# First cross attention: scores of two pairs of heads at a time, or of four

## The reference, cut to what matters

```python
q = _split_heads(Q @ Wq + bq)            # Q: layernorm of x, (16, 64, 512); 16 heads of 32
k = _split_heads(K @ Wk + bk)            # K, V: the context, (16, 512, 512)
v = _split_heads(V @ Wv + bv)
logits = einsum('bhqd,bhkd->bhqk', q, k) / sqrt(32) + mask * -1e9
attn = softmax(logits, axis=-1)
ctx = einsum('bhqk,bhkd->bhqd', attn, v).transpose(0, 2, 1, 3).reshape(Q.shape[0], Q.shape[1], DIM)
return ctx @ Wo + bo
```

## Time and profile before

| what | value |
|---|---|
| time, median of 3 runs (lowest, highest) | 1757.63 us (1753.8, 1759.28) |
| the profiled execution: its own time | 1758.54 us |
| its span in the profile | 1756.8 us |
| its granted TensorE clock, mean | 0.942 of full speed |
| PE busy, DVE busy, ACT busy over the span | 1528.7, 1122.2, 591.7 us |
| first cross attention's main loop | from 92 to 664 us of the span |

### The profile page before, as it was taken

How to read it: one execution, slowest core, us unless ns; L and a number is a source line. 1 busy time by engine, 2 the same in 40 slices (tenths; PEclk the granted TensorE clock), 3 DMA queues, 4 the chain that set the end, 5 groups by cost and what they waited for, 6 DMA issues and landing times. The chain is left out here.

```text
span 1756.8 us, 34069 instructions
## 1 busy us (share of the span) xinstructions
PE 1528.7 (87%) x14116; PEld 996.4 (57%) x14130; DVE 1122.2 (64%) x2155; ACT 591.7 (34%) x1221; POOL 295.8 (17%) x185
## 2 busy tenths in 40 slices
PE   6789999999999994998577899998799995895786
PEld 3567777777777763344545344444466663585343
DVE  3257667676676765521975757675488883765575
ACT  1244443443434442132023110111466662044332
POOL 0400000000000000310010000000499992160000
PEclk9889999999999997899888899998899997998899
DMA  6113122231222204000005000000455421004001
GB/s 231 61 39 132 64 84 86 75 126 70 83 80 90 75 19 158 0 0 1 4 2 198 1 0 0 0 0 0 186 178 191 169 99 35 1 3 145 0 0 48
DMA packets 47909, 120.05 MB, mean 68 GB/s; under 512 B 10605, under 2 KB 15469, under 8 KB 43674
## 3 DMA queue, kind: packets, MB, share of 16 engines
q1 hardware_dynamic: 47770, 118.04, 19.6%
HBM read 100.95 MB, written 17.07 MB: 67 GB/s over the span
## 5 line engine op out<-in xcount | busy, mean ns | idle before, releaser
L1130 POOL TENSOR_TENSOR tm_mixed<-tm_mixed,XNT 128x512 f32<-128x512 f32 x16 | 21.8, 1382 | 662.1 <-DVE tm_mixed L1153 662.1
L617 ACT ACTIVATE l0x_ctxT<-l0x_upper 128x512 fp32r<-128x512 f32 x64 | 40.4, 631 | 237.4 <-DVE l0x_ctxT_lower L700 237.4
L478 PE MATMUL bank<-l0x_ctxT,l0x_upper_k 128*128 128x512 f32 x256 | 104.7, 409 | 5.1 <-ACT l0x_upper_k L627 5.1
L697 DVE TENSOR_SCALAR l0x_upper<-bank 128x512 int32<-128x512 int32 x64 | 44.0, 688 | 95.2 <-PE bank L460 90.6
L478 PE MATMUL bank<-l0x_upper_v,l0x_ctxT 128*128 128x512 f32 x256 | 102.6, 401 | 0.0
L478 PE MATMUL bank<-l0x_ctxT,l0x_lower_k 128*128 128x512 f32 x256 | 101.5, 396 | 0.0
L478 PE MATMUL bank<-l0x_ctxT_lower,l0x_upper_k 128*128 128x512 f32 x256 | 101.4, 396 | 0.0
L478 PE MATMUL bank<-l0x_upper_v,l0x_ctxT_lower 128*128 128x512 f32 x256 | 100.6, 393 | 0.0
L478 PE MATMUL bank<-l0x_lower_v,l0x_ctxT 128*128 128x512 f32 x256 | 100.5, 392 | 0.0
L709 DVE CUSTOM_DVE_ANT_0 l0x_prob<-bank,l0x_mask 128x512 f32<-128x512 f32 x128 | 83.1, 687 | 21.2 <-PE bank L489 20.9
L1043 DVE TENSOR_REDUCE l1x_negmax<-bank 128x1 f32<-128x512 f32 x128 | 82.4, 686 | 21.2 <-PE bank L932 20.8
(11 more groups left out here) (264 smaller groups left out, 3373.5 us busy)
## 6 DMA issues: line engine op xcount, KB each, us to landing
l0x_ctx<-in_ctx SPq DMA_DIRECT2D x16, 1024.0 KB, 5.3
l1x_ctx<-in_ctx SPq DMA_DIRECT2D x16, 1024.0 KB, 5.8
fp_weight<-l0x_weight_piece SPq DMA_DIRECT2D x24, 352.0 KB, 2.4
f_raw<-fp_weight SPq DMA_DIRECT2D x3, 2816.0 KB, 17.4
ternary_weight<-l1x_piece_out SPq DMA_DIRECT2D x24, 256.0 KB, 6.1
f_raw<-ternary_weight SPq DMA_DIRECT2D x3, 2048.0 KB, 14.1
l0x_abs_piece<-in_L_ffn_w_gate SPq DMA_DIRECT2D x8, 512.0 KB, 5.7
l0x_mask<-mask_scratch SPq DMA_DIRECT2D x16, 256.0 KB, 3.6
```

The lines of the kernel that those rows point to most:

```text
L478: last = nc.tensor.matmul(work[bank][:, :], stationary, moving, start=kc == 0 and i == 0, stop=kc == CH - 1 and i == 2)
L697: nc.vector.tensor_scalar(upper.bitcast(I32), work[bank][:, :].bitcast(I32), UPPER_BITS, None, ALU.bitwise_and).then_inc(ctx_upper, 1)
```

## The change

- `scores` issues the four pairs of a half batch at once, on all four row groups: eight products, 16 records, into four banks. It is called in odd steps only. Before, a call had four products and stood in every step.
- The banks come from elsewhere: `score` has four, `probt` one (was two), `pv` one (was two).
- With one `probt` bank, the second pair's four transposes follow the first pair's copy. They are issued behind the step's first projection; ACT's copy, exponential and key copy are interleaved pair by pair likewise.
- `masked_scores` waits once per half batch for scores, and, as PE no longer orders it, for the transposes that read the probabilities which it overwrites.
- With one `pv` bank, `half_product` of step 2 waits for `finish_heads` of the batch before it, not of the one before that.

```diff
-    score, probt, pv, work = g.bank[0:2], g.bank[2:4], g.bank[4:6], g.bank[6:8]
+    score, probt, pv, work = g.bank[0:4], g.bank[4], g.bank[5], g.bank[6:8]
...
-            def scores(b, s):
+            def scores(b, half):
                 par, tokens = b % 2, slice(b * T, (b + 1) * T)
+                if b + half > 0:
+                    pe.wait_ge(masked, (2 * b + half) * 4)
                 for e in range(2):
-                    for i in range(2):
-                        half, r = s // 2, 2 * (s % 2) + i
+                    for r in range(4):
                         rows = slice(32 * r, 32 * r + 32)
-                        last = nc.tensor.matmul(score[i][e * T:(e + 1) * T, :], w.QT[rows, 2 * half + e, tokens],
+                        last = nc.tensor.matmul(score[r][e * T:(e + 1) * T, :], w.QT[rows, 2 * half + e, tokens],
                                                 w.KT[par][rows, 2 * half + e, :], start=True, stop=True)
...
-                        if not (last and u1 == 2):
+                        if s % 2 == 1 and not (last and u1 == 2):
                             if s1 == 0:
                                 pe.wait_ge(key_ready, b0 * CH + CH * (u1 + 1))
-                            pe.wait_ge(masked, n + 2)
-                            scores(b0 + u1, s1)
+                            scores(b0 + u1, s1 // 2)
...
-                                if not first:
-                                    pe.wait_ge(heads_done, b0 + (u - 1))
+                                if not (first and u == 0):
+                                    pe.wait_ge(heads_done, b0 + u)
...
                         for i in range(2):
+                            p = 2 * s + i
                             pe.wait_ge(exp_done, n + (i + 1))
-                            if not (first and u == 0 and s == 0):
-                                pe.wait_ge(probt_ready, n + (i - 1))
+                            if not (first and u == 0 and s == 0 and i == 0):
+                                pe.wait_ge(probt_ready, n + i)
                             for kc in range(KC):
-                                ins = nc.tensor.transpose(probt[i][:, kc * P:(kc + 1) * P],
+                                ins = nc.tensor.transpose(probt[:, kc * P:(kc + 1) * P],
                                                           w.prob[2 * (s % 2) + i][:, kc * P:(kc + 1) * P], g.ident[:, :])
                             ins.then_inc(probt_full, 1)
-                        for p in (2 * s, 2 * s + 1):
                             if ("project", u, p) in uses:
...
-                            nc.scalar.activation(w.PT[r][:, :], probt[i][:, :], ACT.Copy).then_inc(probt_ready, 1)
-                        if not (last and u1 == 2):
-                            exponentials(n + 2, u1 % 2, s1)
-                        for p in (2 * s, 2 * s + 1):
+                            nc.scalar.activation(w.PT[r][:, :], probt[:, :], ACT.Copy).then_inc(probt_ready, 1)
+                            if not (last and u1 == 2):
+                                exponential(n + 2, u1 % 2, s1, i)
                             if ("project", u, p) in uses and p < CH:
...
-                        dve.wait_ge(score_full, m + 1)
+                        dve.wait_ge(score_full, m // 2 + 1)
+                        if m >= 2:
+                            dve.wait_ge(probt_full, 2 * m - 2)
```

More of the change, by code:

```diff
@@ L498, in half_product @@
                             h = head_of(half, e, r)
-                            last = nc.tensor.matmul(pv[par][32 * r:32 * r + 32, (2 * half + e) * T:(2 * half + e + 1) * T],
+                            last = nc.tensor.matmul(pv[32 * r:32 * r + 32, (2 * half + e) * T:(2 * half + e + 1) * T],
                                                     w.V[par][:, kc, h * HD:(h + 1) * HD],
@@ L503, in half_product, with turn_sums @@
                 last.then_inc(half_full, 1)
-            def turn_sums(par):
+            def turn_sums():
                 for half in range(2):
-                    last = nc.tensor.transpose(pv[par][:, 256 + half * P:256 + (half + 1) * P],
+                    last = nc.tensor.transpose(pv[:, 256 + half * P:256 + (half + 1) * P],
                                                w.spread[:, half * P:(half + 1) * P], g.ident[:, :])
@@ L579, in body @@
                             pe.wait_ge(spread_done, b0 + u)
-                            turn_sums(1 - u)
+                            turn_sums()
                         for i in range(2):
+                            p = 2 * s + i
                             pe.wait_ge(exp_done, n + (i + 1))
-                            if not (first and u == 0 and s == 0):
-                                pe.wait_ge(probt_ready, n + (i - 1))
+                            if not (first and u == 0 and s == 0 and i == 0):
+                                pe.wait_ge(probt_ready, n + i)
                             for kc in range(KC):
-                                ins = nc.tensor.transpose(probt[i][:, kc * P:(kc + 1) * P],
+                                ins = nc.tensor.transpose(probt[:, kc * P:(kc + 1) * P],
                                                           w.prob[2 * (s % 2) + i][:, kc * P:(kc + 1) * P], g.ident[:, :])
                             ins.then_inc(probt_full, 1)
-                        for p in (2 * s, 2 * s + 1):
                             if ("project", u, p) in uses:
@@ L604, in body @@
                     pe.wait_ge(spread_done, B)
-                    turn_sums(1)
+                    turn_sums()
                     out_half(2, 2)
@@ L627, in weight_upper, with exponential @@
                 nc.scalar.activation(upper[:, :, :], w.raw_upper[i], ACT.Copy).then_inc(weights_ready, 1)
[L629 to L636, removed]
+            def exponential(n, par, s, i):
+                p = 2 * s + i
+                act.wait_ge(masked, n + (i + 1))
+                prob = w.prob[2 * (s % 2) + i]
+                nc.scalar.activation(prob[:, :], prob[:, :], ACT.Exp, scale=-1.0, bias=w.negmax[:, p:p + 1],
+                                     accum_out=w.rowsum[:, par, p:p + 1]).then_inc(exp_done, 1)
             def sums_copy(par, b):
@@ L641, in sums_copy @@
                 nc.scalar.activation(w.headsT[:, :, par * T:(par + 1) * T],
-                                     pv[par][:, 256:512].rearrange("p (c n) -> p c n", c=CH), ACT.Copy).then_inc(sums_ready, 1)
+                                     pv[:, 256:512].rearrange("p (c n) -> p c n", c=CH), ACT.Copy).then_inc(sums_ready, 1)
             for c in range(CH):
@@ L652, in _ @@
                 context_upper(1, c, CH + c + 1)
-            exponentials(0, 0, 0)
+            for i in range(2):
+                exponential(0, 0, 0, i)
             def body(it, first, last):
@@ L706, in masked_scores @@
                         dve.wait_ge(mask_loaded[par], masks)
-                        dve.wait_ge(score_full, m + 1)
+                        dve.wait_ge(score_full, m // 2 + 1)
+                        if m >= 2:
+                            dve.wait_ge(probt_full, 2 * m - 2)
                     p = 2 * s + i
-                    nc.vector.tensor_tensor_reduce(w.prob[2 * (s % 2) + i][:, :], score[i][:, :], w.mask[par][:, :], 1.0, 3e38,
+                    nc.vector.tensor_tensor_reduce(w.prob[2 * (s % 2) + i][:, :], score[2 * (s % 2) + i][:, :],
+                                                   w.mask[par][:, :], 1.0, 3e38,
                                                    ALU.add, ALU.min, w.negmax[:, p:p + 1]).then_inc(masked, 1)
@@ L725, in finish_heads @@
                 heads = w.headsT[:, :, par * T:(par + 1) * T]
-                nc.vector.tensor_tensor(heads, pv[par][:, 0:256].rearrange("p (c n) -> p c n", c=CH), heads,
+                nc.vector.tensor_tensor(heads, pv[:, 0:256].rearrange("p (c n) -> p c n", c=CH), heads,
                                         ALU.mult).then_inc(heads_done, 1)
```

## The result

The changed kernel takes 1743.49 us (median of 4 runs, 1741.61 to 1744.66), the kernel before 1757.95 (4 runs, 1753.8 to 1759.28): 14.5 us between the medians. The measured ratio is 0.9924 with a 95% interval of 0.9908 to 0.994, which is 13 us faster, give or take 3. Forecast were 1744 and 14 us.

A forecast was written before the change was run, and what follows sets the result against it. The prediction took PE to bound the stage, with DVE's chains covering some steps. Removed 8.2 + 6.1 + 0.3 + 0.7 = 15.3 us, added 1.3, net 14.0: 1744 us, range 1735 to 1752.

The forecast's parts named there:

- A call removed is worth 1.02 where PE sets the time: Scores calls in even steps: each costs PE 1.02 us, gained only where no other engine is nearly as late.
- (0, 2): Step 2 of a body's first batch: 1.44 us slack before, 0.4 after; eight times 1.02, 8.2 us gained.
- (1, 0): Step 0 of a body's second batch, bodies two to seven: six times 1.02, 6.1 us gained.
- rival D: Change does less: value copy in (0, 2) comes late, 8 us go, 1752; chance 0.05.
- (1, 2): Step 2 of a body's second batch: turn waits for DVE's value copy, about 0.9 to 1.0 us; gain 0, seven times.
- (0, 0): Step 0 of a body's first batch: turned sums wait for DVE's spread, about 1.1 us; gain 0, eight times.
- Rival A: PE alone counts, DVE's chains in (1, 2) and (0, 0) shrink: 15.3 us more, 1729, half 1737; chance 0.12.
- The doubled call costs 1.04: Odd steps: a scores call on four row groups takes 1.04 us, 0.02 longer than before.
- A split costs 0.01: Transposes cut in two blocks: 0.01 us each, 53 times where PE counts, 0.5 us added.
- First step 0.3: First step of the stage: scores no longer stand in front of the transposes; 0.3 us gained.
- Last batch 0.7: Last batch, where DVE sets the end: its 0.73 wait of masked scores on scores goes; 0.7 us gained.
- The sum: Whole stage: 15.3 us removed, 1.3 added, net 14.0 us; 1744 predicted.

The follow-up runs named there:

- The experiment that moved the copy: Changed kernel with the first value copy of step (1, 2) moved behind the first of five rounding operations on DVE: 1737.27 us.
- the experiment: Changed kernel with the spread of the row sums computed ahead of the value copies and context parts in step 3: 1740.76 us.
- both moves: Changed kernel with two DVE reorderings, the spread early in step 3 and the first value copy early in (1, 2): 1732.9 us.
- kernel without packs: Changed kernel with scores again called every step for two pairs, single banks and split transposes kept: 1759.23 us, 1.0013 against the kernel before.
- three moves on DVE: Changed kernel with spread early, first value copy of (1, 2) early, and step 3's second value copy behind the context parts: 1743.53 us.

## Why the prediction was right, point by point

- **A call removed is worth 1.02 where PE sets the time.** (0, 2) and (1, 0) lost 1.00 and 0.98, and the table of waits has nothing for them, so the 0.4 us left in (0, 2), rival D's ground, were enough (in one body after, the copy ends at 331.74 and the turn starts at 332.16). Shown.
- **Nothing in (1, 2).** The turn waits 0.95 seven times, as said (0.9 to 1.0). The experiment that moved the copy gave the step 1.11 us back. Shown.
- **Nothing in (0, 0).** The wait is 1.08, eight times (said: 1.1). The working named only the spread; that the context copy stands 0.5 us behind it was worked out only before the experiment, and it limits what can be won there to 0.4 us. Rival A put 15.3 us on the two chains; with both moves made 10.6 came, and most of the rest stands behind the context copy.
- **The doubled call costs 1.04.** It does (353.67 to 354.71). In the loop the odd steps grew by 0.02 to 0.06, which holds this 0.02 and the splits.
- **A split costs 0.01.** The kernel without packs gives 0.01 to 0.02, so 0.5 to 1.1 us for 53 of them. The term that was too small is another: (0, 0) and (1, 2) were put down as exactly unchanged, but they grew by 0.04 and 0.03, some 0.5 us in 15 steps. They grew by as much in the kernel without packs, so it is not the packs. The body takes 71.78 us; 71.7 was said.
- **First step 0.3.** From the first scores to the first transposes the kernel before takes 5.78 us (92.36 to 98.14) and the one after 5.45:

```profile
89.70 2.01 PE L490 MATMUL bank<-l0x_KT,XN 32*64 32x512 f32 x16
95.15 1.11 PE L588 MATMUL bank<-ident,l0x_prob 128*128 128x128 f32 x4 [3.44 <-ACT l0x_prob L634]
```

The difference is 0.33, and it repeats: all nine profiles of kernels with packs have 5.45, the three with scores in every step 5.78 to 5.80. To the first turn it is 0.21 (14.78 against 14.57), but what lies between scatters more than that with the clock (last section), so how much of the 0.33 reaches the end is not shown.

- **Last batch 0.7.** From the last turn to the last turned sums: 59.96 before, 58.20 after: 1.76, the 1.0 of the last (0, 2) and 0.7 to 0.8. In the last batch DVE's masked scores follow its output sum without the 0.73, and PE's waits of 0.78 for ACT's copy are there, hidden as said:

```profile
629.66 0.42 DVE L737 TENSOR_TENSOR X<-X,bank 128x256 f32<-128x256 f32 x1 [0.60 <-PE bank L554]
629.99 0.68 DVE L712 CUSTOM_DVE_ANT_0 l0x_prob<-bank,l0x_mask 128x512 f32<-128x512 f32 x1
...
632.23 0.63 PE L588 MATMUL bank<-ident,l0x_prob 128*128 128x128 f32 x4 [0.78 <-ACT l0x_PT L670]
```

- **The sum.** From the first scores to the last turned sums the profiles have 575.56 and 562.15 us: 13.4, against 14.0 said. The profiled execution itself was 16.2 us faster; 2.7 of these lie ahead of the first instruction that the change touches, and are scatter (below). That the median of 1743.49 lies 0.5 us from the forecast of 1744 is in part luck: the interval is six times as wide on either side. What was right beyond luck is the list of steps that pay and of those that do not.

## What to carry to other kernels

A busy share of 99% on one engine does not say what removing work from it is worth. Take the steps of the loop one by one and ask, for each, how late the second engine's last item is: here 14 of the calls removed paid in full and 15 paid nothing, because what they wait for from DVE had been late by 0.1 us already. A small wait that repeats exactly once a body (here 0.4 and 0.2 us at PE's weight loads) is the sign of such a chain. When work has been taken off the first engine, look at the order of the second one's list: what another engine waits for goes first, what nobody waits for (here, rounding of weights) behind it.

## What was not expected of the hardware

The twelve profiled kernels do the same work up to their first scores of this stage, yet these start between 89.17 and 93.10 us of the span. Single executions can differ by some 4 us from there alone.

A second scatter follows right behind. From the first transposes to the first turn PE does the same work in every kernel that has the split, and yet it takes 7.45 us in the kernel without packs, 8.08 in the one with the three moves on DVE alone and 9.04 to 9.28 in the others. The granted clock tells them apart: it is 0.50 from 92 to 100 us in the kernel after and 0.89 from 100 to 104, while in the kernel without packs it is 0.78 already from 96 to 100. At the low clock the products of a projection start 0.43 us apart, at the full one 0.23. In the kernels with packs they come down to 0.23 between 9.1 and 12.2 us behind the first scores, in the one without packs 7.9 us behind. So a change of a few microseconds in the loop is best read between two points behind the first turn.

And a second pack right behind a first costs 0.87 us, where a pack between other products costs 1.02 to 1.04.
